# Slot-attention iterations: the updates turned one unit sooner, and two small operations moved from ScalarE to VectorE

## The reference

```python
Pn = rmsnorm(P, input_norm_w);  k_proj = Pn @ Wk.T;  v_proj = Pn @ Wv.T
for _ in range(3):
    sn = rmsnorm(slots, slot_norm_w)
    q_proj = sn @ Wq.T
    scores = jnp.einsum('bkd,bmd->bkm', q_proj, k_proj) * SCALE
    attn = jax.nn.softmax(scores, axis=-2)
    attn = attn / (jnp.sum(attn, axis=-1, keepdims=True) + EPS)
    updates = jnp.einsum('bkm,bmd->bkd', attn, v_proj)
    slots = gru_cell(updates, slots, gru_wih, gru_whh, gru_bih, gru_bhh)
```

## Time and profile before

| | us |
|---|---|
| median of 3 runs | 819.0 (817.55 to 820.24) |
| the profiled execution | 818.75 |
| its span in the profile | 816.8 |

### The profile page before, as it was taken

One profiled execution on the slowest core, in us unless ns is written; L12 is line 12 of the kernel. 1 busy time (PEld: TensorE's weight loads), 2 busy tenths in 40 slices (PEclk: granted clock), 3 DMA queues, 4 the chain that ended last, 5 costly groups with the idle time before them and its releaser, 6 DMA issues.

```text
span 816.8 us, 23803 instructions
## 1 busy us (share of the span) xinstructions
PE 691.3 (85%) x8887; PEld 493.4 (60%) x8887; DVE 588.2 (72%) x1092; ACT 537.6 (66%) x1164; POOL 436.6 (53%) x476
## 2 busy tenths in 40 slices
PE   4787999999999999997824678888788875999997
PEld 2255777777777777775512468887777862444443
DVE  4965788788888887886786667778777755566663
ACT  3355677776777777766362599899988962455554
POOL 1859577777777777710000034766656520466664
PEclk9789999999999999999776978999888995899999
DMA  6315544444444444230400504432540531112100
GB/s 197 110 40 164 152 126 133 131 129 131 130 130 130 132 129 132 78 66 14 185 0 1 234 2 157 175 141 85 216 173 2 185 129 38 40 40 78 40 0 23
DMA packets 26543, 85.73 MB, mean 105 GB/s; under 512 B 5780, under 2 KB 7316, under 8 KB 26468
## 3 DMA queue, kind: packets, MB, share of 16 engines
q1 hardware_dynamic: 26472, 84.77, 32.7%
HBM read 65.46 MB, written 0.46 MB: 81 GB/s over the span
## 4 chain that ended last, share of the span: by engine, by line
PE 46%; DVE 17%; POOL 16%; issue 8%; ACT 7%; SPq 3%; DMA 2%; POOLq 0%; DVEq 0%; ACTq 0%
POOL ctx_lo L614 8%; PE ps L1352 8%; PE ps L1369 7%; PE ps L1383 7%; PE ps L1339 4%; PE ps L1616 3%; ACT c_prob L779 3%; PE ps L1328 2%; PE ps L1600 2%; PE ps L1388 2%; SPq L439 2%; DVE ps L1173 2%; DVE tile_max L865 1%; DVE amax_part L1089 1%; ACT w0T L779 1%
## 5 line engine op out<-in xcount | busy, mean ns | idle before, releaser
L865 DVE TENSOR_REDUCE tile_max<-ps 128x1 f32<-128x500 f32 x336 | 215.1, 675 | 51.3 <-PE ps L1352 50.4
L640 ACT ACTIVATE probs<-ps 125x896 f32<-125x896 f32 x192 | 175.3, 916 | 95.2 <-PE ps L1369 94.4
L1352 PE MATMUL ps<-k_hi,qdiag 128*128 128x500 f16 x336 | 130.9, 392 | 6.9 <-DVE tile_max L865 5.7
L779 ACT ACTIVATE c_prob<-ps,c_bias,row_scale 125x56 f32<-125x56 f32 x384 | 116.4, 475 | 6.8 <-DVE c_bias L1176 6.8
L614 POOL TENSOR_TENSOR ctx_lo<-ctx_hi,ctx_lo 128x448 f16<-128x448 f32 x64 | 72.1, 1128 | 72.5 <-ACT ctx_lo L823 72.5
L1369 PE MATMUL ps<-qstack,kstack 98*125 98x224 f16 x768 | 107.2, 263 | 0.4
L578 POOL TENSOR_TENSOR c_prob<-c_prob,c_weight 125x672 f32<-125x672 f32 x32 | 42.0, 1313 | 118.3 <-DVE c_weight L1190 118.3
L1369 PEld LDWEIGHTS ps<-qstack,kstack 98*125 98x125 f16 x768 | 86.6, 137 | 21.4 <-ACT probs L640 3.3
L1600 PE MATMUL ps<-query_hi,ctx_hi 128*128 128x56 f16 x576 | 55.8, 194 | 34.5 <-ACT c_prob L779 24.8
L1383 PE MATMUL ps<-probs,v_aug 125*32 125x168 f32 x1536 | 75.4, 314 | 3.3 <-ACT probs L640 2.5
L1656 PE MATMUL ps<-ctx_lo 128*128 128x448 f16 x192 | 68.9, 359 | 6.7 <-DVE ctx_hi L1287 3.0
(11 more groups left out here) (268 smaller groups left out, 1728.2 us busy)
## 6 DMA issues: line engine op xcount, KB each, us to landing
row_tiles<-in_ctx_rows_wide SPq DMA_DIRECT2D x40, 774.0 KB, 5.6
ctx<-in_ctxT SPq DMA_DIRECT2D x16, 750.0 KB, 5.3
rows_in<-in_ctx_rows SPq DMA_DIRECT2D x16, 750.0 KB
kstack<-k_hi SPq DMA_DIRECT2D x128, 93.8 KB, 2.7
kstack<-k_lo SPq DMA_DIRECT2D x64, 93.8 KB, 2.7
ctx_hi<-in_wg SPq DMA_DIRECT2D x8, 256.0 KB, 2.6
ctx_hi<-in_wu SPq DMA_DIRECT2D x8, 256.0 KB, 3.0
ctx_hi<-in_wd SPq DMA_DIRECT2D x8, 256.0 KB, 3.4
```

The lines of the kernel that those rows point to most:

```text
L640: nc.scalar.activation(probs[c % RING_P][0:CH, :].rearrange("p (k w) -> p k w", k=2), score_tile(c)[0:CH], ACT.Exp, scale=float(HD) ** -0. ...
L779: last = nc.scalar.activation(c_prob[n % PROBS][:, c, :], ps[0:CH, 2 * (n % 2) + c // 6, bass.ts(c % 6, TOK)], ACT.Exp, bias=c_bias[n % 2] ...
L865: nc.vector.reduce_max(tile_max[:, u % MAXT, u // MAXT:u // MAXT + 1], ps[:, MAXB + (u + p) % 2, 0:KCOLS], AX.X).then_inc(max_done, 1)
L1352: nc.tensor.matmul(ps[:, MAXB + (u + p) % 2, 0:KCOLS], qdiag[p][:, bass.ts(t, 128)], k_hi[p][:, bass.ts(j, KCOLS)], start=True, stop=True) ...
```

## The change

The transpose of a quad's updates moves from number 35 to 31, from the last slot of u0 to the last slot of u3, one unit sooner. The copy of the result to SBUF, number 31 as before, is now VectorE's. The rounding of the queries to half precision leaves ScalarE too: VectorE does it right behind the scaling that it depends on, and waits for its own semaphore in between.

```diff
-        TENSOR_AT = dict(sums=(19, 27), turn=35, gates=39, means=51)
-        SCALAR_AT = dict(copy=31, tanh=38, cand=41, hi=57)
-        VECTOR_AT = dict(rows=27, hidden=41, slots=45, root=49, scaled=57, lo=58)
+        TENSOR_AT = dict(sums=(19, 27), turn=31, gates=39, means=51)
+        SCALAR_AT = dict(tanh=38, cand=41)
+        VECTOR_AT = dict(rows=27, copy=31, hidden=41, slots=45, root=49, scaled=57, lo=58)
...
-            def updates_out(g):
-                act.wait_ge(u_turned, g + 1)
-                wait(act, gates_ready, g)
-                nc.scalar.copy(updT.rearrange("p (b t) -> p b t", b=QUAD),
-                               ps[:, TURN, 0:2 * D].rearrange("p (b t) -> p b t", b=QUAD)[:, :, 0:TOK]).then_inc(u_copied, 1)
-
...
-            def query_high(g):
-                act.wait_ge(r_slots, g + 1)
-                nc.scalar.activation(query_hi[:, quad(g)], projected, ACT.Copy, scale=norm_w[:, 1:2]).then_inc(qc_hi, 1)
-
...
+            def updates_out(g):
+                dve.wait_ge(u_turned, g + 1)
+                wait(dve, gates_ready, g)
+                nc.vector.tensor_copy(updT.rearrange("p (b t) -> p b t", b=QUAD),
+                                      ps[:, TURN, 0:2 * D].rearrange("p (b t) -> p b t", b=QUAD)[:, :, 0:TOK]).then_inc(u_copied, 1)
+
...
             def scaled_queries(g):
                 dve.wait_ge(r_inv, 2 * g + 2)
                 nc.vector.tensor_tensor(projected, projected, rs_y[:], ALU.mult).then_inc(r_slots, 1)
+                dve.wait_ge(r_slots, g + 1)
+                nc.vector.tensor_scalar(query_hi[:, quad(g)], projected, norm_w[:, 1:2], None, ALU.mult).then_inc(qc_hi, 1)
```

More of the change, by code:

```diff
@@ L801, in candidate @@
                 nc.scalar.activation(new_cand, gru_t[:, 2, :], ACT.Tanh, bias=gru_b[:, 2:3]).then_inc(cand_done, 1)
-            def query_high(g):
-                act.wait_ge(r_slots, g + 1)
-                nc.scalar.activation(query_hi[:, quad(g)], projected, ACT.Copy, scale=norm_w[:, 1:2]).then_inc(qc_hi, 1)
-            iterations(unit, [(SCALAR_AT["copy"], False, updates_out), (SCALAR_AT["tanh"], False, gates),
-                              (SCALAR_AT["cand"], False, candidate), (SCALAR_AT["hi"], True, query_high)], unit_last=True)
+            iterations(unit, [(SCALAR_AT["tanh"], False, gates), (SCALAR_AT["cand"], False, candidate)], unit_last=True)
             load_table(ACT.Sqrt)
@@ L1256, in _ @@
             iterations(unit, [
-                (VECTOR_AT["rows"], False, update_rows), (VECTOR_AT["scaled"], True, scaled_queries), (VECTOR_AT["hidden"], False, hidden_part),
+                (VECTOR_AT["rows"], False, update_rows), (VECTOR_AT["copy"], False, updates_out), (VECTOR_AT["scaled"], True, scaled_queries), (VECTOR_AT["hidden"], False, hidden_part),
                 (VECTOR_AT["slots"], False, new_slots), (VECTOR_AT["slots"], True, slot_squares), (VECTOR_AT["root"], True, root_guess),
```

## The result

The changed kernel takes 823.84 us (median of 12 executions, 821.66 to 826.49), the kernel before in the same session 819.91 (12, 817.55 to 821.12). The ratio is 1.0053, with a 95% interval of 1.0041 to 1.0065: slower, by 3.9 us by the medians and 4.3 by the ratio. The profiled execution takes 822.85 us with a span of 820.8, 4.1 and 4.0 more than before.

What follows compares the result with a forecast made beforehand. The slot stage was taken to be bound by VectorE and GpSimd in turn, not ScalarE. Terms +5.5, -0.6 and -0.5 gave +4.4 us, or 823.1 on the profiled execution; forecast 823.2, 8-in-10 range 820.3 to 825.6.

Steps and rivals of the forecast that it cites:

- What bounds the stage: Slot stage: VectorE without a gap from scaling to guess (8.61 us), then GpSimd to the next scaling, rounds of 17.3 to 17.5.
- The rival in which ScalarE was the bound: Slot rounds: VectorE has room for both operations, and the path through ScalarE and TensorE shortens; about 811 us, chance 0.07.
- The two operations: VectorE, scaling to guess: the rounding adds 0.48 us a round and the copy 0.31, over seven rounds +5.5.
- The ring: First to eighth guess, seven rounds of VectorE then GpSimd: +5.5 us for the new operations, -0.6 in two TensorE-held halves.
- ends with GpSimd in every round: Half from guess to scaling: stays at 8.7 to 8.9 us, with GpSimd last; two TensorE-held halves lose 0.6 in total.
- Outside the ring: Before the first guess and behind the eighth: transpose and ScalarE copy go, VectorE operations and later gates add; together -0.5 us.
- The gates' wait for the copy behind the new slots: Drain: the last gates wait for VectorE's copy, queued behind the new slots, and start about 0.3 us later.
- Cheap operations and a warm TensorE: Rival: both operations at low bounds, and the transpose in TensorE's idle time keeps its clock up; about 821.2 us, chance 0.17.
- the forecast's own range: Whole kernel: 822.6 to 824.8 us around 823.2, by the bounds of the two VectorE operations; chance 0.66.

## Why the prediction held, point by point

*What bounds the stage.* Right. A VectorE operation placed between scaling and guess costs its pitch in every round (8.61 to 8.91, to 9.11, to 9.40); the same copy on the other side of the guess costs the ring nothing (121.74 against 121.91); and taking away ScalarE's 1.16 us of waiting leaves the half at 8.61. The rival in which ScalarE was the bound, at about 811 us, is refuted by the transpose alone, which ends ScalarE's wait and shortens no half by more than 0.06 us but the two that TensorE held.

*The two operations.* 0.48 and 0.31 a round were predicted, 0.49 to 0.51 and 0.30 measured, together 0.79 against 0.79. Neither waited for anything unforeseen. A rule of the Trainium skill (Perfetto Trace Analysis, "Optimizing Scalar/DVE Operations") says that work of a saturated VectorE may go to ScalarE; here the reverse move cost 0.27% and 0.67%, so by that rule the trace agrees, though VectorE was not saturated by its share (77% of the ring) but only in one half of each round.

*The ring.* +4.9 us was predicted (+5.5 and -0.6), +5.02 measured. The halves from scaling to guess grew by 5.3 in sum, a little less than 5.5 because two of them had been 8.79 and 8.67. The halves from guess to scaling lost 0.28, not 0.6. Here a step failed: **"ends with GpSimd in every round"**. One round of seven (9.64 us) ends with TensorE, whose sums ran at a granted clock of 0.57. The prediction had taken the excess of the two rounds before for a matter of instructions, and it is mostly one of the clock: their sums took 3.39 and 3.75 us, against 2.88 in others.

*Outside the ring.* -0.5 was predicted. From the stage's start to the first guess it came out at +0.08 (46.58 against 46.50) and the tail at -2.15, so the term was mis-sized. In front of the first guess the transpose's 0.49 did go, and 0.25 of it came back as longer sums (3.50 against 3.25 us). Of the tail's -2.15, 1.66 is the last gates at the full clock (2.57 against 4.23). The gates' wait for the copy behind the new slots was right: they start 2.05 after the last division (676.03, L1200), against 1.71 before, +0.34 for the predicted +0.3. What is left of the tail, -0.83, is near the -0.59 of its other terms; a set of sums that is on the chain before and takes 3.98 us there, and 3.24 in the changed kernel, can have given at most 0.74 of it. These are the last division, the copy and the gates:

```profile
676.03 0.42 DVE u_rows L1200
...
677.22 0.40 DVE stream L1226
677.64 0.40 DVE work L1205
678.08 0.65 PE ps L1631 x2
```

So the stage as a whole grew by 2.9 us in the profiles, not by 4.4. The 1.66 us of the last gates, a level of the clock for which the prediction had no term, are as much as the difference. Another 1.2 us lie ahead of the slot stage (it starts at 462.22 instead of 461.01), where the program is the same: that is scatter between executions, for in the twelve profiles the stage starts anywhere from 457.8 to 463.2. That the total of the profiled execution (+4.1 us) comes so near the predicted +4.4 is therefore in part luck. The +3.9 us of the medians rest on 12 executions each.

*The parts by themselves.* By the terms on record the transpose alone was worth about -1.6 us, the copy +2.5 and the rounding +3.5. The ratios give -3.4, +2.2 and +5.5, each with an interval of about +-1.4 to +-1.8. The transpose and the rounding are both on the far side, with opposite signs, and the sum is right. The stage's own lengths say less: -1.87 for the transpose, of which -1.12 in the ring and -0.99 in the tail. In its profiled execution another 1.3 us lie ahead of the stage and 0.9 behind it, where the program is the same. Where the other 1.5 us of the transpose's -3.4 come from is not settled.

*Cheap operations and a warm TensorE.* The prices were not at their low end. Nor did the transpose in the idle time keep the clock up in general. One round ahead of the first guess (logits from 489.94, and from 488.70 before) the logits of u0 take 1.86 us with it and 1.87 without, and over the ring the granted clock is 0.87, against 0.89. The Trainium skill (TensorE: Matmul & The Clock Gate, Part 1) says that activity releases the throttle; a transpose of some 0.4 us did not do so there.

*Slips in the sums.* The upper end of the forecast's own range is 824.6 by its terms (818.75 + 0.25 + 6.7 - 0.6 - 0.5), not 824.8, and with the 0.25 that the rivals were given the forecast would be 823.4, not 823.2. Neither matters for the outcome.

## What to carry to other kernels

Cut a loop that runs over several engines at the places where they hand over to each other, and ask for each half which engine has no gap in it: the busiest engine by share (ScalarE, 90% of the ring) may have slack, while one with 77% has none in its own half. A half without a gap makes an engine a candidate and no more (ScalarE had such halves too once the transpose was moved); what decides is to take work off it or put work on it and to see whether the half moves. In VectorE's half an operation of 0.3 us costs 0.3 us a round, and the same operation on the other side of the handover is free. When the bound is moved, look first at the ends of the loop and at which engine is next: three of the ten variants here did in one half what was expected of them and lost it elsewhere, to a queue in two of them and in part to TensorE's clock in the third. And a tail or a stretch that differs by 1 or 2 us between two single profiles may be the clock, so compare its instructions' durations before giving it a cause.

## What the runs showed of the hardware

The granted clock of TensorE makes the same instructions take quite different times within one execution: 48 sums 2.88 us at 1.00, 3.51 at 0.81 and 4.89 at 0.57; the 12 gate matmuls 2.57 at 1.00 and 4.23 at 0.60. In the kernel before, the low level comes once a round, in or just behind TensorE's idle time before u0 (2.2 to 3.2 us). With the transpose in that idle time it mostly still does, but one round of the changed kernel (logits of u0 from 541.91) has idle times of 1.6, 0.4 and 0.6 us and no low level behind them. Whether it falls on the logits of u0 or on the sums differs between rounds and between kernels, and none of the edits here explains it. In a chain in which TensorE holds half of each round, that is worth more (0.64 us) than the transpose itself (0.47).
